# Two lanes taken by each engine in an order of its own, with hand-offs by half a group

## What is computed

```python
x = _layernorm(x + _L0_attn_ref(x, ...))    # gated recurrence, a scan along the tokens
x = _layernorm(x + _L0_xattn_ref(x, ctx))   # 16 heads of 8, 64 context words
x = _layernorm(x + _L0_ffn_ref(x, ...))     # fake-quantised, one scale for the whole of x
x = _layernorm(x + _L1_attn_ref(x, ...))    # segments of 64, and every 4th word of 4 neighbours
x = _layernorm(x + _L1_xattn_ref(x, ctx, masks))   # 16 heads of 64
x = _layernorm(x + _L1_ffn_ref(x, ...))     # 8 experts, the 512 best tokens of each
x = _layernorm(x + _L2_attn_ref(x, ...))    # long convolution, gated
x = _layernorm(x + _L2_xattn_ref(x, ctx, ctx))
x = _layernorm(x + _L2_ffn_ref(x, rhs))     # int8 product, one scale per token
x = _layernorm(x + _L3_attn_ref(x, ...))    # retention, 16 heads, causal decay mask
x = _layernorm(x + _L3_xattn_ref(x, ctx, ...))  # cross attention, self attention, gelu layer
x = _layernorm(x + _L3_ffn_ref(x, ...))     # ternary weights: 128 -> 512 -> 512 -> 512 -> 128
```

## Time and profile before

| | us |
|---|---|
| runs | 3220.93, 3225.58, 3229.11 |
| median | 3225.58 |
| the profiled execution | 3235.79 |
| its span in the trace | 3233.8 |
| PE busy | 2542.1 (79%) |
| PE weight loads | 1797.2 (56%) |
| DVE busy | 1690.1 (52%) |
| ACT busy | 998.0 (31%) |
| POOL busy | 355.6 (11%) |

### The profile page before, as it was taken

The page is one execution under the profiler, slowest core; times in us unless marked ns, Lnnn a source line. Parts: engine busy times, 40 slices in busy tenths (PEclk is TensorE's granted clock), DMA queues, the critical chain, the costliest instruction groups (busy, mean ns, idle before and its releaser), DMA issues.

```text
span 3233.8 us, 51781 instructions
## 1 busy us (share of the span) xinstructions
PE 2542.1 (79%) x22430; PEld 1797.2 (56%) x22430; DVE 1690.1 (52%) x4079; ACT 998.0 (31%) x1389; POOL 355.6 (11%) x605
## 2 busy tenths in 40 slices
PE   4666468888888887886677789777897777987778
PEld 3444156777777776664555455554555555555454
DVE  5666735656665654603376532665426654176541
ACT  4444312222232222031233432324323243232432
POOL 0111000111001100073110001100011000010000
PEclk8887559999999998897899999989999998998999
DMA  2000000000000000225400000000000000000000
GB/s 85 1 1 3 0 1 2 8 8 8 1 8 8 8 8 14 86 42 111 128 1 1 1 7 1 1 1 1 7 1 1 1 1 7 1 1 1 1 1 26
DMA packets 39349, 48.06 MB, mean 15 GB/s; under 512 B 7169, under 2 KB 36369, under 8 KB 38354
## 3 DMA queue, kind: packets, MB, share of 16 engines
q1 hardware_dynamic: 33490, 40.43, 4.2%
q0 software_dynamic: 5632, 4.33, 1.0%
HBM read 31.82 MB, written 12.91 MB: 14 GB/s over the span
## 4 chain that ended last, share of the span: by engine, by line
PE 55%; DVE 29%; ACT 7%; issue 4%; POOL 3%; DMA 1%; SPq 0%; DVEq 0%; another core or an unknown queue 0%; POOLq 0%; ACTq 0%
PE banks L2408 7%; DVE wide_area L2284 5%; PE banks L2609 4%; PE banks L878 3%; DVE wide_area L1758 2%; PE banks L1378 2%; PE banks L2182 2%; PE banks L2397 2%; PE banks L870 2%; PE banks L1177 2%; DVE weights L2101 2%; PE banks L1343 2%; PE banks L1411 1%; PE banks L1685 1%; DVE xs L907 1%
## 5 line engine op out<-in xcount | busy, mean ns | idle before, releaser
L2609 PE MATMUL banks<-wA 128*128 128x128 f32 x2664 | 368.0, 292 | 4.0 <-ACT xf L939 2.1
L2609 PEld LDWEIGHTS banks<-wA 128*128 128x128 f32 x2664 | 341.6, 205 | 22.5 <-issue 15.4
L899 DVE BATCH_NORM_STATS2 stats<-banks 128x6 f32<-128x128 f32 x208 | 46.2, 284 | 338.6 <-PE banks L878 315.1
L2284 DVE TENSOR_REDUCE wide_area<-banks 128x8 f32<-128x2048 f32 x64 | 146.7, 2293 | 105.0 <-PE banks L2182 105.0
L914 POOL TENSOR_TENSOR rstd<-moments,eps 128x4 f32<-128x4 f32 x56 | 11.2, 199 | 1417.6 <-DVE moments L903 1417.1
L2265 ACT ACTIVATE weights<-banks 128x2048 f32<-128x2048 f32 x64 | 120.1, 1877 | 102.4 <-PE banks L2191 102.4
L1758 DVE TENSOR_REDUCE wide_area<-banks 128x16 f32<-128x1024 f32 x80 | 94.1, 1218 | 46.1 <-PE banks L1671 45.6
L1724 ACT ACTIVATE weights<-banks 128x2048 f32<-128x2048 f32 x32 | 59.6, 1876 | 99.0 <-PE banks L1685 99.0
L2408 PE MATMUL banks<-wide_area,big 128*128 128x512 f32 x192 | 85.7, 592 | 0.0
L2101 DVE TENSOR_TENSOR weights<-banks,wC 128x2048 f32<-128x2048 f32 x32 | 72.2, 2286 | 22.7 <-PE banks L1988 22.7
L914 POOL TENSOR_TENSOR smalls<-smalls,eps 128x4 f32<-128x4 f32 x16 | 3.2, 199 | 727.9 <-DVE smalls L903 727.9
(11 more groups left out here) (765 smaller groups left out, 5964.4 us busy)
## 6 DMA issues: line engine op xcount, KB each, us to landing
big<-in_wE SPq DMA_DIRECT2D x1, 4096.0 KB, 12.6
weights<-long_kernel SPq DMA_DIRECT2D x8, 512.0 KB, 7.6
conv<-wide_area SPq DMA_DIRECT2D x16, 256.0 KB, 3.1
wC<-in_wC SPq DMA_DIRECT2D x1, 3012.0 KB, 15.2
wC<-in_wG SPq DMA_DIRECT2D x1, 2971.0 KB, 20.4
big<-in_wT SPq DMA_DIRECT2D x1, 2560.0 KB, 11.1
x_all<-in_xT SPq DMA_DIRECT2D x1, 2048.0 KB, 8.2
total<-spread SPq DMA_DIRECT2D x8, 256.0 KB, 2.3
```

What stands on the lines that cost most here:

```text
L899: dve.bn_stats(m.stats[:, i, :], self.tokens(i)).then_inc(*sg.up("dve", f"stats{i}"))
L2284: return dve.tensor_reduce(m.peaks[:, k % 2, :, :].rearrange("p t (r c) -> p r t c", r=4)[:, :, :, SPARE[j]], m.bank[:, :, :].rearrange("p ...
L2609: pe.matmul(bank[:, 0:P], m.ident, m.ident, start=True, stop=True)
```

## The change

1. **Orders.** `FIRST`, `MIDDLE`, `LAST` and `weave` go. `ORDERS` has a string of its own for each stage and each engine. For `last` it runs over all four rounds at once (`rounds` strings a lane's rounds together): 1432 letters on PE, 952 on DVE, 1158 on ACT, 818 on POOL. Most sections get more places to stop (`yield`), one behind almost each wait.
2. **z by pairs of tiles.** z of tiles 0 and 1 is built in bank 3 and that of tiles 2 and 3 in bank 1 (`z_tile`), each with its own semaphore step; the norm's statistics start on the first pair. `by_half` does a section's first product on each half as it comes out of the norm. `gathered` opens z of tiles 0 and 2 with all terms but the last, before the last term is ready.
3. **Hand-offs by bank.** Exponentials in `LaneCross` and `LaneSegment` in two instructions of 1024 columns, and the values' products in two parts behind them. The mask of `Retention` in two parts, with the scores of bands 2, 3 and 1 of a tile issued before DVE has centred the tile before, and band 0 behind it; the normalising of a tile is moved one tile later. `TokenQuant` by halves, without the pass that took the rounding constant off (ACT's copy does it with a bias). `SelfLayer`'s end by tiles.
4. **Unread products** only in choice and experts.

The diff, cut to its core (the order strings shortened to their beginning; the functions around it are printed above):

```diff
-def weave(ahead, behind, ticks, lag=LAG):
...
-LAST = "nnfnnfnfnfnfnfnfnfnfnfnfnfnfnffnnnfnffnfnfnfn...
+BUSY = {'taken': 20, 'chosen': 5, 'choice start': 8, 'choice same': 4, 'choice bit': 3, 'choice rank': 40}
+ORDERS = {
...
+    "last": {
+        "pe": "nnffnnnfnnnnnffffffnfnnfnnfnffnfnfnnnfnnffnffnffffn...
+        "dve": "nnffnnnfffnnfnnfnfffnnnnnnffffffnnnnnnfffnfffnfnfn...
...
+Z_BANKS = (3, 1)
+def z_tile(bank, i):
+    return bank[:, Z_BANKS[i // 2], i % 2 * P:(i % 2 + 1) * P]
...
+def gathered(pe, sig, bank, turned, ident, terms, last_ready):
+    def opening(i):
+        laid(pe, z_tile(bank, i), turned[:, i * P:(i + 1) * P], ident)
+        for left, right in terms[:-1]:
+            pe.matmul(z_tile(bank, i), left[:, i * P:(i + 1) * P], right, start=False, stop=False)
+    opening(0)
+    opening(2)
+    yield
+    pe.wait_ge(*last_ready)
+    left, right = terms[-1]
+    for half, _, tiles in HALVES:
+        for i in tiles:
+            if i % 2:
+                opening(i)
+            mm = pe.matmul(z_tile(bank, i), left[:, i * P:(i + 1) * P], right, start=False, stop=True)
+        mm.then_inc(*sig.up("pe", half + "z"))
...
     def dve(self, dve, n, z_ready):
         m, sg = self.lane, self.sig
-        dve.wait_ge(*z_ready)
-        for i in range(NT):
-            dve.bn_stats(m.stats[:, i, :], self.tokens(i)).then_inc(*sg.up("dve", f"stats{i}"))
+        for (_, _, tiles), ready in zip(HALVES, z_ready):
+            dve.wait_ge(*ready)
+            for i in tiles:
+                dve.bn_stats(m.stats[:, i, :], self.tokens(i)).then_inc(*sg.up("dve", f"stats{i}"))
+            yield
...
-        m.keep_busy(pe, m.bank[:, 1, :], self.place)
...
             act.wait_ge(*sg.done("pe", f"turned{b}", n))
-            act.activation(m.weights, wide, ACT.Exp, scale=DK ** -0.5).then_inc(*sg.up("act", f"exp{b}"))
+            for k, step in enumerate(("first_exp", "exp")):
+                part = slice(k * 1024, (k + 1) * 1024)
+                act.activation(m.weights[:, part], wide[:, part], ACT.Exp, scale=DK ** -0.5).then_inc(*sg.up("act", f"{step}{b}"))
...
         for i in range(NT):
-            if i:
+            if i == 0:
+                scores(i, (2, 3)).then_inc(*sg.up("pe", f"upper{i}"))
+                scores(i, (0, 1)).then_inc(*sg.up("pe", f"scores{i}"))
+            else:
+                scores(i, (2, 3, 1)).then_inc(*sg.up("pe", f"upper{i}"))
+                yield
                 pe.wait_ge(*sg.done("dve", f"centre{i - 1}", n))
...
-            for it in range(ITERS // 2):
-                turns(lane_pe(pe, 0, it), lane_pe(pe, 1, it), LAST)
+            turns(rounds(lane_pe, pe, 0), rounds(lane_pe, pe, 1), ORDERS["last"]["pe"])
```

More of the change, by code:

```diff
@@ L814 @@
-BUSY = {'first1': 2, 'dil_sum0': 7, 'wide scores1': 8, 'lead norm': 10, 'near norm': 1, 'dil_peaks1': 12, 'dil_peaks0': 2, 'lead product': 5, 'wide start': 2, 'gate': 7, 'back0': 3, 'first3': 1, 'first0': 1, 'first norm': 5, 'last norm 0': 9, 'last norm 1': 12, 'last norm 2': 9, 'last norm 3': 12, 'last norm 4': 12, 'last norm 5': 8, 'last norm 7': 1, 'last norm 8': 8, 'retention turned': 7, 'quant whole': 2, 'taken': 20, 'chosen': 5, 'choice start': 8, 'choice same': 4, 'choice bit': 3, 'choice rank': 40}
@@ L946, in act, with out @@
         yield
+    def out(self, n):
+        return [self.sig.done("act", half + "out", n) for half, _, _ in HALVES]
 class ExpertSum:
@@ L1906, in pe @@
[L1906 to L1915 removed]
+        pe.wait_ge(*x_ready[-1])
```

724 lines of the change are left out of this document (435 added, 289 removed).

## The result

The changed kernel takes 3087.9 us (median of four runs, 3086.3 to 3092.6), the kernel before 3227.4 us beside it. The ratio is 0.9575, with a 95% interval of 0.9559 to 0.9592: 4.3% faster, where 7.4% was forecast. The sign and the range held; of the gain came 60%.

A forecast was written before the change was run, and what follows sets the result against it. Dependence inside a lane, lengthened by service to and waits for the other lane, was the bound. Gains of 170 last, 60 middle, 25 first, 3 ends, less 20 clock, made 238: 2988 us; range 2870 to 3160.

The forecast's parts named there:

- Unread products: Removing them from PE's chain gains 45 us: 20 in last, 20 in middle, 5 in first; ends 0 and 110.
- The clock: In last and middle, PE's share at half speed grows by a few hundredths, costing 20 us; ends 0 and 95.
- The clock rival: Same gains of 258 us, but clock 0.85 in last and middle takes 95 back: 3063 us; chance 0.14.
- Seams: In last, one lane's ternary layers overlap the other's work where rounds meet: 15 us each, 60 for four.
- Instructions held back: Engines no longer wait for one lane while the other's work is ready: 45 us last, 20 middle, 12 first.
- DVE's waits before statistics: Sign over the span, 315.1 + 82.8 us before: staying above 300 us would show the lanes stay together.
- Hand-offs: Passing exponentials, norms, retention and others on by halves gains 45 us in last, 20 in middle, 8 in first.
- ends: Outside the three stages, a norm and a sum by halves gain 3 us.
- Middle's step: Sign in middle: one step near 95 us for 104, with PE busy about 0.8 of it.
- The second rival: Lanes don't come apart; seam and held-back gains fall to nothing, about 100 us left: 3126 us; chance 0.12.
- the slower case: Clock 0.77 in all of last and middle, 306 us more PE time, all on the path: 3274 us; chance 0.10.
- the rival of more than forecast: Half of the DVE waits on the path instead of 77 us, some 110 us more gain: 2878 us; chance 0.10.

The follow-up runs named there:

- b_no_products: Kernel before with unread products left only in choice and experts, orders and hand-offs as before: 3351.5 us, ratio 1.0397.
- a_seams_closed: Changed kernel with last's orders rearranged so each engine finishes a round of both lanes before the next: 3164.3 us, ratio 0.9867.
- a_alternate: Changed kernel with last's four orders replaced by plain alternation of the two lanes, piece by piece: 3300.5 us, ratio 1.0270.
- a_mid_fit: Changed kernel with unread products added in middle only, at places where its trace shows PE idle: 3051.4 us, ratio 0.9493.
- a_near_norm: Changed kernel with unread products in middle only before the near lane's norm transposes: 3062.0 us, ratio 0.9509.
- a_fit_both: Changed kernel with unread products at two places in middle and three calls before each norm's transposes in last: 3060.7 us, ratio 0.9504.
- a_middle_products: Changed kernel with middle's unread products put back at the old places; 618 of 870 rows came back: 3086.4 us, ratio 0.9586.
- a_last_products: Changed kernel with last's unread products put back before the norms' and retention's transposes: 3165.7 us, ratio 0.9809.
- a_again: Changed kernel unaltered, run again as the mark for others on its chip: 3090.5 us, ratio 0.9602 to the kernel before.
- a_whole_parts: Changed kernel with three finer waits made whole (exponentials, masks' scores, norm's last half), orders kept: 3228.3 us, ratio 1.0015.
- a_mask_whole: Changed kernel with both of retention's masks of a tile waiting for all the tile's scores: 3133.2 us, ratio 0.9747.
- a_exps_half: Changed kernel with exponentials and the norm's last half awaited as wholes, masks' finer hand-off kept: 3179.0 us, ratio 0.9879.

## Why the prediction was right or wrong

The forecast was a gain of 238 us in the profiled execution; it is 143.

**Unread products, forecast +45: the step that failed.** Taken away alone, they cost 117 us (span 3350.7 against 3233.8): middle -75, last -39, first -4 where I had +20, +20, +5. The ends were 0 and 110, so the sign that came wasn't in the range of the term; not even with the clock's worst end, 95 us lost, do the two terms reach it. The reason given was sound as far as it went (products on the chain, about 139 us, give way to the wait behind them), but it priced only PE's time.

**The clock, forecast -20: the same failure seen from the other side.** I judged the clock by how closely PE would be packed, and took single stretches for witnesses, self attention at 0.94 and retention at 0.77. The rows of the stages held a hint: middle had the most products for its length and 0.94, first few and 0.76. It was no proof, since last, with fewer than middle for its length, stood at 0.96, and first had less useful work too. Together the two terms were +25 and came to -117, 142 us of error.

The clock rival had the mechanism right and, for the two terms together, too small a price: 0.85 in both stages, 95 us. What came is 0.81 in middle and 0.93 in last, so it holds in the one stage and not in the other. The rule of the Trainium skill that I put beside it (page TensorE: Matmul & The Clock Gate, Part 1) spoke for it, and b_no_products shows that it should have had more than 0.14.

**Seams, 60 in last: right in sum**, 60 to 85 by a_seams_closed, but 14, 7 and 55 us over three seams for 15 at each of four. The picture behind it was only partly right: the lanes' ternary layers come apart with other work between them in one round of the first three. Self attention comes apart in rounds two, three and four, where the other lane's first scores are 34 to 43 us behind the first lane's. In the first round the lanes go side by side, 4.6 us apart where it was 12.5:

```profile
1735.50 1.15 PE L2353 MATMUL banks<-keys,qf 32*128 32x256 f32 x16 [0.24 <-ACT value_area L2450]
...
1740.14 1.15 PE L2353 MATMUL banks<-spread,gates 32*128 32x256 f32 x16 [0.47 <-ACT spread L2450]
```

In the second round the scores, L2353, in stretches of 20 us:

```profile
2090.00:2110.00 20.00, 2.29 (x32) 1.50 (x32) 0.74 0.00 1
2110.00:2130.00 20.00, 2.19 (x32) 1.54 (x32) 1.00 0.01 2
2130.00:2150.00 20.00, 4.15 (x64) 3.08 (x64) 1.00 0.00 1
2150.00:2170.00 20.00, 4.60 (x69) 3.09 (x64) 1.00 0.01 2
2170.00:2190.00 20.00, 3.23 (x32) 1.94 (x32) 0.74 0.00 1
2190.00:2210.00 20.00, 1.74 (x28) 1.30 (x32) 1.00 0.06 14
```

Two units at a time in the middle, one at the ends: one lane's first units run beside the other's cross attention, and the other's last units beside the first lane's feed-forward part and sum.

**Instructions held back, 45 + 20 + 12.** Not priced by a run of its own. The gap between root and scaling shrank by 48.5 us over last's norms, the longest from 5.5 to 3.6, and DVE's waits before statistics by 129 us in the whole (147 in last); the case of the earlier trace rows is gone.

**Hand-offs, 45 + 20 + 8.** Undone in part, with the orders kept, 83 to 107 in last, 20 to 26 in middle, 13 to 14 in first. In middle and first about as forecast; in last twice, with the reservation above. In last the shares found by undoing one thing are 60 to 85 for seams and 83 to 107 for hand-offs, 143 to 192 of a whole of 153 before anything held back is counted, and a_alternate alone is 202 to 227 longer. So the parts rest on one another and can't be added.

**The parts together** (orders and hand-offs, without products on both sides): last 153 for 150 forecast, middle 65 for 40, first 37 for 20, ends 3.5 for 3. 259 for 213, so these terms were 46 us too small. 238 - 142 + 46 = 142, which is the 143 measured. That the range held owes something to luck: it was 290 us wide, and the two errors went opposite ways. The forecast's middle was also the 730 us of the earlier trace rows, seven steps, and what is measured here is all of it, 902 us and eight steps, so part of what middle gave over its terms is only that.

**The other signs named.** Middle's step, by the chain's pieces of L1454 (454.61 to 1103.03 us, six steps), is 108 us, not 95 and longer than the 104 before; PE's share is 730.7 of 910.8, 0.80, as forecast, but it is slow rows that fill it. Last is 1537 us for 1480. The clock in last held, 0.93. DVE's waits before statistics are under 300 us, the sign named for lanes that come apart. The second rival, lanes that don't, is out, since it had the seams at nothing and they are 60 to 85; so is the slower case, which needed 0.77 in all of both stages. In the rival of more than forecast, half of the 397.9 us of waits less the 77 us of terms is 122 us, not some 110.

How much the omission of the products costs in the changed kernel is less than 117 us: 36 us could be had back in middle (a_mid_fit), nothing in last, where the new orders alone brought the clock from 0.90 to 0.93 and fill the waits with work.

## What to carry to other kernels

Before taking unread work off TensorE, sum it up by stage beside that stage's granted clock, and price its removal with the rows at both rates, not as freed time. After any change of order test the fillers again: a filler belongs where the new trace has PE idle or its clock low, and the old places may have become real work's places. A change that reorders and removes fillers at once should be timed in both halves, since here they were worth +259 and -117 us.

## What was not expected of the hardware

In middle each microsecond of products returned about one microsecond of useful PE time by the clock, and in last less. In middle of the changed kernel, with useful time 727.6 without any: 19.3 us of products return 21.6 (a_near_norm), 41.2 return 53.9 (a_fit_both), 99.3 return 81.6 (a_middle_products); in the kernel before, 127.4 returned 121.9. In last 163.9 returned 98 in the kernel before, and 164.8 returned 37 to 72 in the changed one (a_last_products, against the five profiles of the same last). What is returned is not yet time gained: 9 to 11 us of middle in a_middle_products, a loss in a_last_products.

Two profiles of one code can differ in their clock with DVE's and ACT's work the same: last at 0.94 and at 0.91 (a_again, a_mid_fit, on two chips) is 1527.3 and 1551.8 us long, PE 1229.2 and 1263.5 us busy. A lower clock also went along with added waits: 0.86 in a_alternate, 0.89 in a_whole_parts, 0.90 in a_mask_whole, all under the 0.91 to 0.94 of the same code unaltered; a_seams_closed and a_exps_half, at 0.91, are at its lower end. So part of what a bad order costs may be paid in clock; how much of those 200 us, these runs don't tell.
